# Delta attention: a new order of the engines' steps within the slots, and the transposed keys one slot sooner

## The chip, the cores and the metric

The kernel runs on one core of one Trainium2 chip. Its time is the device time of one execution in microseconds (us). The kernel before took 6605.63 us as the median of three runs (6602.77 to 6611.05). PE is TensorE, PEld its weight load, DVE VectorE, ACT ScalarE, POOL GpSimd.

## The reference, cut to what matters

The program computes four transformer layers on 2048 tokens of width 256, all in fp32, each with an attention and a feed-forward part. The change touches only the attention of layer 0, a gated delta rule with 16 heads of 128 x 128 state:

```python
q = short_conv(x @ Wq.T, conv_q); k = short_conv(x @ Wk.T, conv_k); v = short_conv(x @ Wv.T, conv_v)
v_hat = k @ Wsv.T; e = v_hat - v                        # statistics: |e|2, |e|1, cosine
beta = sigmoid(mlp_b(s)); amp = mlp_a(s)                # 3 -> 32 -> 1
g = -exp(A_log) * softplus(r * amp + dt_bias)           # decay of every key channel
...
def step(S, inp):
    S = S * exp(g_t)[..., None]
    delta = (v_t - k_t @ S) * b_t
    S = S + k_t[..., None] * delta[..., None, :]
    return S, q_t * scale @ S
...
o = rmsnorm(o) * norm_w * sigmoid(x @ Wg1.T @ Wg2.T + bg2);  return o @ Wo.T
```

## The kernel before, in words

`delta_attention` cuts the work into 64 units: a head times a group of 512 tokens, which is four chunks of 128. Units are software-pipelined. Each engine runs the same Python loop over slots `for g in range(SLOTS)`, and a new unit enters every `SL = 7` slots. `at(g, OFF)` says which unit has the step of offset `OFF` in slot `g`, so a step always falls on the same remainder of `g` by 7. I call these remainders slot 0 to slot 6. A unit passes through some 34 slots, so about five units are in work at once.

What runs in which slot (offset modulo 7):

- Projections K, V, Q on PE (L296): slots 0, 1, 2. ACT copies each out of the PSUM bank twice (L492, L493), and DVE adds the three other taps of the convolution (`convolve`, L680) in slots 1, 2, 3.
- Slot 4 silu; slot 5 values transposed (L328) and v_hat (L336), squares on ACT (L517 to L519, L582 to L584), errors on DVE (L764, L793); slot 6 the sums of squares on PE (`STAT`, L383); slot 0 `SUMS`, transposes of the sums (L431).
- Slot 1 `ROOT`: DVE copies the sums out (L704 to L706) and POOL takes a power of 128x20 numbers (L642). Slots 2, 3, 4: the small MLPs, on POOL and DVE.
- Slot 6 `Z`: PE spreads a and beta (L360, L366), DVE makes z and the scaled keys kF (L729, L737), ACT a softplus argument. Slots 0 and 1: DVE evaluates a polynomial (`horner`, L694). Slot 2 `KQ`: the decay (L527, L726), decayed keys and queries (POOL L635, DVE L740), their diagonal (L352, L752).
- Levels 0 to 6 in slots 3, 4, 5, 6, 0, 1, 2: the 128 x 128 triangular inverse is built by doubling. In each level PE forms `products` (L305), DVE masks them into MA (L691), POOL scales kq, kF and tot (`scale`, L614 to L616), PE multiplies (L396), ACT copies Xs (L569), PE multiplies again (L437, in the last level L439), DVE subtracts into Tm (L831), PE transposes Tm (L310) and ACT copies TT (L512). In level 0, Tm comes from a transpose (L451, L785), and two levels of `products` run in slot 3, one before and one behind `scale(ul, 0)`.
- Chunks k = 0 to 3 in slots 3 to 6, the recurrence: W (L341, reads the state St), R (DVE L770, ACT L508 for the first chunk of a sequence), D (L424), its copy Dl (ACT L552), S (L466) with O (L462, L467), and the new St (DVE L842 or L844). The S of chunk 0 also reads `khat`, the transposed keys (`KH`, PE L376, ACT L549), in slot 3.
- Slot 0 `OUT` (ACT L589, DVE L825, PE L476), slot 1 the root of the mean square (POOL L663), slot 3 `Y`, the output projection (PE L417) with its four copies on ACT (L560). Slot 3 `GATE`: the gate's matmul (L323), read by ACT in slot 4 (L544).

The order of the steps within a slot is the order in which the source has them; nothing reorders them afterwards. Each engine takes its instructions strictly in that order, so one that waits on a semaphore holds up all behind it. Weights come by DMA once for every four units, into two buffers.

Of the kernel before, what the change touches and what calls it, by code (L numbers as in the profile page):

```python
# [10 lines left out]
ALU = mybir.AluOpType  # L11
ACT = mybir.ActivationFunctionType
# [167 lines left out]
GATE_AT, KH_AT, CHUNK_AT, OUT_AT, RMS_AT, Y_AT = 17, 24, 24, 28, 29, 31  # L180
# [7 lines left out]
def delta_attention(nc, T, ins):  # L188
    with ExitStack() as c:
# [76 lines left out]
        with nc.Block() as block:  # L266
# [18 lines left out]
            def _(pe):  # L285
# [27 lines left out]
                for g in range(SLOTS):  # L313
# [4 lines left out]
                    if (u := at(g, GATE_AT)) is not None:  # L318
                        pe.wait_ge(evac[2], min(u + 3, NU0))
                        pe.wait_ge(z_ready, u + 1)  # L320
                        if u:
                            pe.wait_ge(tg_ready, u)
                        nc.tensor.matmul(fr[:, 1, :], w_of(u)[:, W_G2:W_END], g1T[:, tok(u):tok(u) + GRP], start=True, stop=True).then_inc(tg_mm, 1)  # L323
# [13 lines left out]
                    if chunk and not (first(uc) and k == 0):  # L337
                        if k == 0:
                            pe.wait_ge(scaled, 7 * uc + 7)
                        pe.wait_ge(s_ready, 4 * uc + k)  # L340
                        nc.tensor.matmul(ca[:, 0:P], kq[:, uc % 2, 0, ch_(k)], St[:, uc % 2], start=True, stop=True).then_inc(w_mm, 1)  # L341
                    if (u := at(g, K_AT)) is not None:
                        pe.wait_ge(*w_loaded(u))
                        if u:
                            pe.wait_ge(vtok_ready, u)
                        project(u, 1, W_K, 0)
                    if (u := at(g, KQ_AT)) is not None:
                        pe.wait_ge(kF_ready, u + 1)
# [93 lines left out]
                    if (u := at(g, V_AT)) is not None:  # L442
                        if u >= 2:
                            pe.wait_ge(z_ready, u - 1)
                        if u == 1:
                            pe.wait_ge(evac[2], 1)
                        project(u, 2, W_V, 1)
                    if level and lv == 0:
                        pe.wait_ge(mask0_ready, ul + 1)
                        for j in range(NC):  # L450
                            last = nc.tensor.transpose(xy[:, ch_(j)], MA[:, 0, ch_(j)], T.ident[:])  # L451
# [1766 lines left out]
```

## Time and profile before

| | |
|---|---|
| median of three runs | 6605.63 us |
| profiled execution, its own time | 6588.47 us |
| its span, first to last instruction | 6586.7 us |
| delta attention within it | about 24 to 3140 us |
| PE, PEld busy over the span | 92%, 67% |
| DVE, ACT, POOL busy over the span | 59%, 41%, 35% |
| mean granted TensorE clock | 0.959 of 2.4 GHz |

Busy time is the sum over the whole program, so its shares average over nine stages. For this change only the first half of the span matters, and in it the repeating unit: the same 7 slots come round 64 times. A timeline row gives the start, the length, the engine and the line, and in brackets how long the engine was idle before it and who ended that. A PE busy time is that of pipelined matmuls, whose ends are modelled, so the starts are the better clock.

### The profile page before, as it was taken

To read this page: it belongs to the slowest core of one execution; us is meant where nothing else is said; L and a number is where in the kernel's file an instruction comes from. 1 tells how busy PE (TensorE), PEld (TensorE's weight loads), DVE (VectorE), ACT (ScalarE), POOL (GpSimd) and SP (SyncE) were. 2 spreads that over 40 slices of the span, in tenths; PEclk is the share of its full clock that TensorE was granted. 3 is DMA by queue.
4 is the path that set the end of the run, shared out by engine and by line. 5 is a ranking of instruction groups with operands and counts; after the bars stand their busy time and mean duration, and the time that the engine had idled before them with its cause. 6 is when DMAs were issued, how large, how long until landed. Compare 5 with 4: busy or idle time off the path is not lost. (4 is left out here: it accounts for less than half of the span.)

```text
span 6586.7 us, 99233 instructions
## 1 busy us (share of the span) xinstructions
PE 6069.7 (92%) x37522; PEld 4392.9 (67%) x37522; DVE 3858.4 (59%) x7222; ACT 2708.2 (41%) x5584; POOL 2308.8 (35%) x2602
## 2 busy tenths in 40 slices
PE   5898989898889898988899999999999989999999
PEld 3777777777777777777477777653334667767665
DVE  5777777777777777775334444337654444444322
ACT  4445454545454444443145555413664122222211
POOL 3666667676666666675000000010000011111100
PEclk8999999999999999999999999998999999999999
DMA  0000000000000000000000000000001011211200
GB/s 29 5 5 5 3 2 5 5 5 5 5 5 1 5 5 5 5 1 1 15 18 14 12 11 12 23 7 1 1 1 52 1 62 62 68 68 68 75 7 7
DMA packets 33925, 112.56 MB, mean 17 GB/s; under 512 B 4272, under 2 KB 9648, under 8 KB 33456
## 3 DMA queue, kind: packets, MB, share of 16 engines
q1 hardware_dynamic: 33456, 106.22, 4.8%
q8 instruction: 305, 5.00, 0.3%
q14 instruction: 164, 1.34, 0.1%
HBM read 104.11 MB, written 2.10 MB: 16 GB/s over the span
## 5 line engine op out<-in xcount | busy, mean ns | idle before, releaser
L614 POOL TENSOR_TENSOR d_kq<-d_kq,d_tot 128x512 f32<-128x512 f32 x448 | 556.6, 1242 | 829.2 <-PE d_lpd L305 823.8
L305 PE MATMUL d_lpd<-d_kq,d_kF 128*128 128x128 f32 x3584 | 550.2, 302 | 110.9 <-POOL d_tot L616 103.3
L680 DVE SCALAR_TENSOR_TENSOR d_qkv<-d_raw,d_wts,d_qkv 128x512 f32<-128x512 f32 x576 | 506.8, 888 | 124.8 <-ACT d_qkv L493 120.0
L305 PEld LDWEIGHTS d_lpd<-d_kq,d_kF 128*128 128x128 f32 x3584 | 491.1, 211 | 133.1 <-POOL d_tot L616 126.5
L691 DVE COPY_PREDICATED d_MA<-d_pairs,d_lpd 128x512 f32<-128x512 int32 x384 | 316.4, 824 | 359.6 <-PE d_lpd L305 356.9
L396 PEld LDWEIGHTS d_xy<-d_Tm,d_MA 128*128 128x128 f32 x3072 | 409.4, 205 | 167.4 <-issue 165.7
L396 PE MATMUL d_xy<-d_Tm,d_MA 128*128 128x64 f32 x3072 | 434.8, 288 | 58.8 <-ACT d_TT L512 57.4
L1744 DVE TENSOR_REDUCE r_nm<-r_ps 128x2 f32<-128x1024 f32 x256 | 307.8, 1223 | 138.6 <-PE r_ps L1563 138.4
L994 POOL TENSOR_TENSOR f1rstd<-f1var,mhalf 128x4 f32<-128x4 f32 x4 | 4.0, 1009 | 1097.1 <-DVE f1var L1019 1097.1
L296 PE MATMUL d_fr<-xnT,d_wts 128*128 128x512 f32 x768 | 380.1, 618 | 0.7 <-ACT d_g1T L487 0.7
L437 PE MATMUL d_xy<-d_Xs,d_TT 128*128 128x64 f32 x2560 | 366.9, 293 | 0.2 <-ACT d_Xs L569 0.2
L1841 PE MATMUL e_pj<-xnT,e_wts 128*128 128x512 f32 x768 | 347.7, 602 | 13.5 <-DMA e_wts<-in_w3all 11.7
L437 PEld LDWEIGHTS d_xy<-d_Xs,d_TT 128*128 128x128 f32 x2560 | 358.4, 216 | 0.4 <-ACT d_Xs L569 0.4
L615 POOL TENSOR_TENSOR d_kF<-d_kF,d_tot 128x256 f32<-128x256 f32 x448 | 352.0, 786 | 0.0
L1664 ACT ACTIVATE r_pT<-r_ps 128x512 f32<-128x512 f32 x512 | 274.9, 598 | 146.3 <-PE r_ps L1571 145.7
L694 DVE SCALAR_TENSOR_TENSOR d_lp<-d_lp,d_ez 128x512 f32<-128x512 f32 x448 | 325.0, 725 | 13.1
L512 ACT ACTIVATE d_TT<-d_xy 128x256 f32<-128x256 f32 x320 | 124.5, 389 | 464.3 <-PE d_xy L310 464.3
L1304 DVE TENSOR_TENSOR c_sc<-c_sc,c_mask 128x128 f32<-128x128 f32 x256 | 76.7, 300 | 397.8 <-PE c_sc L1181 397.8
L1219 PEld LDWEIGHTS c_po<-c_pT,c_vt 128*128 128x128 f32 x2304 | 294.7, 191 | 21.0 <-ACT c_pT L1279 9.3
L1219 PE MATMUL c_po<-c_pT,c_vt 128*128 128x128 f32 x2304 | 301.9, 276 | 0.2
L1563 PE MATMUL r_ps<-r_kT,r_qT 32*128 32x512 f32 x1024 | 292.1, 694 | 2.7 <-DVE r_nm L1744 1.1
L642 POOL TENSOR_TENSOR d_pw<-d_st,d_half 128x20 f32<-128x20 f32 x64 | 257.5, 4024 | 98.6 <-DVE d_sums L706 98.5
(399 smaller groups left out, 13919.4 us busy)
## 6 DMA issues: line engine op xcount, KB each, us to landing
e_wts<-in_w3all SPq DMA_DIRECT2D x64, 897.0 KB, 4.6
d_wts<-in_headw SPq DMA_DIRECT2D x16, 583.5 KB, 3.8
c_wqo<-in_wqo SPq DMA_DIRECT2D x32, 256.0 KB, 2.6
f3ws<-in_f3w SPq DMA_DIRECT2D x17, 384.0 KB, 8.2
f2ws<-in_f2s SPq DMA_DIRECT2D x16, 256.0 KB, 6.6
f2qs<-in_f2q SPq DMA_DIRECT2D x16, 256.0 KB, 6.8
f1ws<-in_f1w SPq DMA_DIRECT2D x8, 384.0 KB, 6.4
f0ws<-in_f0w SPq DMA_DIRECT2D x6, 384.0 KB, 5.4
```

The costliest lines, as they stand in the source:

```text
L296: last = nc.tensor.matmul(fr[:, bank, :], w_of(u)[:, w0 + kd * P:w0 + (kd + 1) * P], T.xnT[:, kd, tok(u):tok(u) + GRP], start=(kd == 0), s ...
L305: last = nc.tensor.matmul(out[:, :, k], kF[:, u % 2, ch_(k)], moving[:, :, k, :, 1], start=True, stop=True)
L396: last = nc.tensor.matmul(mh(xy[:, j * 64:(j + 1) * 64], h), MA[:, lv, ch_(j)], even(Tm[:, ch_(j)], h), start=True, stop=True)
L437: last = nc.tensor.matmul(xy[:, 256 + j * 64:256 + (j + 1) * 64], TT[:, ul % 2, ch_(j)], Xs[:, j * 64:(j + 1) * 64], start=True, stop=True)
L614: nc.gpsimd.tensor_tensor(v, v, bc(bc(t_l[:, :, 0], 2, h), 1, 2), ALU.mult)
L615: nc.gpsimd.tensor_tensor(f, f, bc(t_l[:, :, 1], 2, h), ALU.mult)
L680: step = nc.vector.scalar_tensor_tensor(qkv[:, u % 3, x], raw[:, u % 2, x, i:i + GRP], tap(u, x, i), qkv[:, u % 3, x], ALU.mult, ALU.add)
L691: nc.vector.copy_predicated(into, bc(mh(pairs[:, lv], h), 1, 2), lpd[:].rearrange("p (x m h) -> p x m h", x=2, h=h)).then_inc(masked, 1)
L694: ch.link(nc.vector.scalar_tensor_tensor(lp[:], lp[:], LOG1P[i], ez[:], ALU.add, ALU.mult))
L1219: last = nc.tensor.matmul(po[:, 0:P], vt[:, n // (4 * QT) % 2, j], pT[:, n % 2, j * P:(j + 1) * P], start=(j == 0), stop=(j == t))
L1744: nc.vector.tensor_reduce(nm[:, t % 2, half, 4 * j + i0:4 * j + i0 + 2], ps[:, row_pair(row - 1):row_pair(row - 1) + 2], AX, ALU.max).then ...
L1841: last = nc.tensor.matmul(pj[:, x % 2, :], w[:, w0 + kd * P:w0 + (kd + 1) * P], T.xnT[:, kd, g * GRP:(g + 1) * GRP], start=(kd == 0), stop ...
```

## The change

`KH_AT` goes from 24 to 23: the four transposes of the scaled keys run in slot 2, behind the level 6 multiply and ahead of the projection of Q, and no longer in slot 3. ACT copies them out at the head of slot 3. All else moves steps within their slot. In each engine's loop the blocks stand in another order; their contents, waits, operands and buffers are as before. POOL's blocks move too, but since each runs in only one slot of the seven, the sequence of POOL's instructions comes out the same as before. No instruction is added or removed on any engine.

```diff
-GATE_AT, KH_AT, CHUNK_AT, OUT_AT, RMS_AT, Y_AT = 17, 24, 24, 28, 29, 31
+GATE_AT, KH_AT, CHUNK_AT, OUT_AT, RMS_AT, Y_AT = 17, 23, 24, 28, 29, 31
...
             def _(pe):
-                    if (u := at(g, GATE_AT)) is not None:
-                        pe.wait_ge(evac[2], min(u + 3, NU0))
...
+                    if (u := at(g, STAT_AT)) is not None:
+                        pe.wait_ge(kq_sq, u + 1)
+                        pe.wait_ge(err_sq, u + 1)
...
             def _(act):
-                    if (u := at(g, CHUNK_AT)) is not None:
-                        act.wait_ge(kh_mm, u + 1)
...
+                    if (u := at(g, Y_AT)) is not None:
+                        act.wait_ge(yo_mm, u + 1)
...
+                    if chunk:
+                        act.wait_ge(dl_mm, 4 * uc + k + 1)
+                        nc.scalar.activation(Dl[:, ch_(k)], ca[:, 0:P], ACT.Copy).then_inc(dl_ready, 1)
...
             def _(dve):
+                    if (u := at(g, K_AT + 1)) is not None:
+                        convolve(u, 1, 2)
...
                     if level and lv < 6:
                         mask(ul, lv + 1)
...
+                    if chunk:
+                        dve.wait_ge(s_mm, 4 * uc + k + 1)
...
+                    if (u := at(g, Z_AT)) is not None:
+                        nc.vector.tensor_tensor(kF[:, u % 2], qkv[:, u % 3, 1], fr[:, 2, :], ALU.mult).then_inc(kF_ready, 1)
```

The first place is DVE from the end of slot 6 through slot 0 into slot 1. Before, from the start of the polynomial (d_lp) to the second tap of K (d_qkv):

```order
L734 TENSOR_SCALAR d_lp<-d_ez 128x512
L694 SCALAR_TENSOR_TENSOR d_lp<-d_lp,d_ez 128x512 x3
L691 COPY_PREDICATED d_MA<-d_pairs,d_lpd 128x2x8x32
L825 SCALAR_TENSOR_TENSOR d_og<-d_tg,d_co 128x512
L694 SCALAR_TENSOR_TENSOR d_lp<-d_lp,d_ez 128x512
L831 TENSOR_TENSOR d_Tm<-d_Tm,d_xy 128x16x16
L704 TENSOR_SCALAR d_st<-d_fr 128x16
```

And now, where the line numbers are those of the changed file (L742 is L734, L817 is L825, L824 is L831):

```order
L742 TENSOR_SCALAR d_lp<-d_ez 128x512
L694 SCALAR_TENSOR_TENSOR d_lp<-d_lp,d_ez 128x512 x4
L691 COPY_PREDICATED d_MA<-d_pairs,d_lpd 128x2x8x32
L817 SCALAR_TENSOR_TENSOR d_og<-d_tg,d_co 128x512
L824 TENSOR_TENSOR d_Tm<-d_Tm,d_xy 128x16x16
L704 TENSOR_SCALAR d_st<-d_fr 128x16
```

The fourth step of the polynomial has moved from between d_og and d_Tm to ahead of the mask d_MA.

The second place is PE in slot 3 of a unit whose chunks carry a state over, from the last multiply of level 6 to the W of chunk 1. Before:

```order
L439 MATMUL d_xy<-d_TT,d_Xs 64x64 x4
L323 MATMUL d_fr<-d_g1T,d_wts 128x512
L341 MATMUL d_ca<-d_St,d_kq 128x128
L376 MATMUL d_fr<-ident,d_kF 128x128 x4
L305 MATMUL d_lpd<-d_kq,d_kF 128x2x64 x4
L417 MATMUL d_fr<-d_wo,d_og 128x256 x4
L424 MATMUL d_ca<-d_R,d_TT 128x128
L451 MATMUL d_xy<-ident,d_MA 128x128 x4
L305 MATMUL d_lpd<-d_kq,d_kF 128x2x64 x4
L462 MATMUL d_co<-d_kq,d_St 128x128
L466 MATMUL d_ca<-d_Dl,d_khat 128x128
L467 MATMUL d_co<-d_MA,d_Dl 128x128
```

And now, where L433 is L439, L369 is L341, L398 is L417, L405 is L424, L461 is L451:

```order
L414 MATMUL d_fr<-ident,d_kF 128x128 x4
L296 MATMUL d_fr<-xnT,d_wts 128x512 x2
L433 MATMUL d_xy<-d_TT,d_Xs 64x64 x4
L369 MATMUL d_ca<-d_St,d_kq 128x128
L305 MATMUL d_lpd<-d_kq,d_kF 128x2x64 x4
L398 MATMUL d_fr<-d_wo,d_og 128x256 x4
L405 MATMUL d_ca<-d_R,d_TT 128x128
L442 MATMUL d_co<-d_kq,d_St 128x128
L446 MATMUL d_ca<-d_Dl,d_khat 128x128
L447 MATMUL d_co<-d_MA,d_Dl 128x128
L461 MATMUL d_xy<-ident,d_MA 128x128 x4
L305 MATMUL d_lpd<-d_kq,d_kF 128x2x64 x4
```

The transposed keys (L414) now stand ahead of the projection of Q, and O and S of chunk 0 (L442 to L447) ahead of the second `products`. The gate's matmul, L477, is the next row behind these; it was the first of slot 3 (L323).

The third place is DVE in the same slot. Before, from the first mask to the new state:

```order
L749 COPY_PREDICATED d_MA<-d_pairs,d_lpd 128x256
L770 SCALAR_TENSOR_TENSOR d_R<-d_vtok,d_pw,d_ca 128x128
L777 TENSOR_TENSOR d_TT<-ident,d_MA 128x512
L782 COPY_PREDICATED d_MA<-d_pairs,d_lpd 128x256
L785 TENSOR_TENSOR d_Tm<-ident,d_xy 128x512
L680 SCALAR_TENSOR_TENSOR d_qkv<-d_raw,d_wts,d_qkv 128x512 x2
L691 COPY_PREDICATED d_MA<-d_pairs,d_lpd 128x2x128x2
L817 COPY d_raw<-d_raw 128x3x3
L844 SCALAR_TENSOR_TENSOR d_St<-d_St,d_tot,d_ca 128x128
```

And now:

```order
L716 COPY_PREDICATED d_MA<-d_pairs,d_lpd 128x256
L680 SCALAR_TENSOR_TENSOR d_qkv<-d_raw,d_wts,d_qkv 128x512
L737 COPY_PREDICATED d_MA<-d_pairs,d_lpd 128x256
L754 SCALAR_TENSOR_TENSOR d_R<-d_vtok,d_pw,d_ca 128x128
L680 SCALAR_TENSOR_TENSOR d_qkv<-d_raw,d_wts,d_qkv 128x512
L778 TENSOR_TENSOR d_TT<-ident,d_MA 128x512
L680 SCALAR_TENSOR_TENSOR d_qkv<-d_raw,d_wts,d_qkv 128x512
L798 TENSOR_TENSOR d_Tm<-ident,d_xy 128x512
L691 COPY_PREDICATED d_MA<-d_pairs,d_lpd 128x2x128x2
L830 SCALAR_TENSOR_TENSOR d_St<-d_St,d_tot,d_ca 128x128
L838 COPY d_raw<-d_raw 128x3x3
```

The three taps of Q (L680) are now strung between the masks and the two differences from the identity, and the copy of the halo (d_raw) stands behind the state.

## Rows read from the trace of the kernel before

**Rows 1.** Busy time and granted clock (PEclk) of four stretches, all engines.
```profile
400.00:2800.00 2400.00, 2158.92 (x14615) 1775.58 (x14616) 1845.17 (x3522) 1157.39 (x2343) 1640.89 (x1886) 0.94 0.01 4
1512.70:1519.50 6.80, 6.24 (x26) 5.75 (x27) 5.35 (x9) 0.77 (x2) 6.51 (x7) 0.50 0.01 2
1536.60:1540.00 3.40, 3.40 (x18) 3.40 (x17) 2.20 (x8) 1.72 (x4) 0.42 (x1) 0.50 0.04 10
1567.00:1656.00 89.00, 79.22 (x564) 63.84 (x564) 70.86 (x136) 45.26 (x92) 63.14 (x73) 1.00 0.03 8
```

**Rows 2.** What PE waited for, 400 to 2800 us: total, times, longest.
```profile
PE d_lpd L305 <- POOL d_tot L616: 81.8, 50, 2.6
PE d_xy L396 <- ACT d_TT L512: 43.9, 101, 0.6
PE d_ca L341 <- DVE d_St L842: 41.9, 25, 2.0
PE d_ca L341 <- DVE d_St L844: 38.4, 26, 1.9
PE d_xy L310 <- DVE d_Tm L831: 33.6, 51, 0.8
```

**Rows 3.** POOL's power, once in each unit: count, lengths, first and last start.
```profile
L642 POOL TENSOR_TENSOR d_pw<-d_st,d_half x64: 3523/4042/4044, 71.9 to 3030.3; 128x20 f32<-128x20 f32 x64
```

**Rows 4.** Timeline of one unit, slots 0 to 2: start, length, line, idle before.
```profile
1606.95 0.94 DVE L694 SCALAR_TENSOR_TENSOR d_lp<-d_lp,d_ez 128x512 f32<-128x512 f32 x1
1607.93 0.42 DVE L831 TENSOR_TENSOR d_Tm<-d_Tm,d_xy 128x256 f32<-128x256 f32 x1
1608.40 0.66 PE L310 MATMUL d_xy<-ident,d_Tm 128*128 128x128 f32 x4 [0.66 <-DVE d_Tm L831]
1608.66 4.04 POOL L642 TENSOR_TENSOR d_pw<-d_st,d_half 128x20 f32<-128x20 f32 x1 [0.70 <-DVE d_sums L706]
1609.62 1.08 PE L396 MATMUL d_xy<-d_Tm,d_MA 128*128 128x64 f32 x8 [0.56 <-ACT d_TT L512]
1613.53 0.41 DVE L831 TENSOR_TENSOR d_Tm<-d_Tm,d_xy 128x256 f32<-128x256 f32 x1
1614.10 0.60 PE L310 MATMUL d_xy<-ident,d_Tm 128*128 128x128 f32 x4
1615.89 1.08 PE L396 MATMUL d_xy<-d_Tm,d_MA 128*128 128x64 f32 x8 [0.30 <-ACT d_TT L512]
```

**Rows 5.** Timeline of the same unit, slot 3 and the head of slot 4.
```profile
1619.18 1.27 POOL L635 TENSOR_TENSOR d_kq<-d_qkv,d_tot 128x512 f32<-128x512 f32 x1
1619.28 1.12 PE L323 MATMUL d_fr<-d_g1T,d_wts 128*128 128x512 f32 x2
1620.41 0.72 POOL L646 TENSOR_TENSOR d_hid<-d_hid 128x256 f32<-128x256 f32 x1
1620.90 1.07 PE L305 MATMUL d_lpd<-d_kq,d_kF 128*128 128x128 f32 x8
1621.21 2.18 POOL L647 TENSOR_TENSOR d_hid<-d_hid,d_mlp 128x256 f32<-128x256 f32 x1
1621.40 1.40 DVE L680 SCALAR_TENSOR_TENSOR d_qkv<-d_raw,d_wts,d_qkv 128x512 f32<-128x512 f32 x2
1624.44 1.56 ACT L560 ACTIVATE d_y<-d_fr,d_rr 128x256 f32<-128x256 f32 x4
1626.84 0.38 PE L305 MATMUL d_lpd<-d_kq,d_kF 128*128 128x128 f32 x1 [2.18 <-POOL d_tot L616]
1628.29 1.29 DVE L691 COPY_PREDICATED d_MA<-d_pairs,d_lpd 128x512 f32<-128x512 int32 x1
1629.79 0.49 PE L341 MATMUL d_ca<-d_St,d_kq 128*128 128x128 f32 x2 [1.10 <-DVE d_St L844]
```

**Rows 6.** Timeline of the same unit, slots 5 and 6, the statistics.
```profile
1638.97 0.64 ACT L584 ACTIVATE d_sqs<-d_sqs 128x512 f32<-128x512 f32 x1
1641.48 1.92 PE L383 MATMUL d_fr<-d_sqs,d_pick 128*32 128x512 f32 x14
```

More of the change, by code:

```diff
@@ L441, in _ @@
                         last.then_inc(yt_mm, 1)
[L442 to L451, printed above, removed]
-                        last.then_inc(tr_mm, 1)
-                        pe.wait_ge(scaled, 7 * ul + 1)
-                        pe.wait_ge(masked, 7 * ul + 1)
-                        products(ul, 1)
                     if chunk:
@@ L477, in _ @@
                         last.then_inc(ss_mm, 1)
+                    if level and lv == 0:
+                        pe.wait_ge(mask0_ready, ul + 1)
+                        for j in range(NC):
+                            last = nc.tensor.transpose(xy[:, ch_(j)], MA[:, 0, ch_(j)], T.ident[:])
+                        last.then_inc(tr_mm, 1)
+                        pe.wait_ge(scaled, 7 * ul + 1)
+                        pe.wait_ge(masked, 7 * ul + 1)
+                        products(ul, 1)
+                    if (u := at(g, V_AT)) is not None:
+                        if u >= 2:
+                            pe.wait_ge(z_ready, u - 1)
+                        if u == 1:
+                            pe.wait_ge(evac[2], 1)
+                        project(u, 2, W_V, 1)
+                    if (u := at(g, GATE_AT)) is not None:
+                        pe.wait_ge(evac[2], min(u + 3, NU0))
+                        pe.wait_ge(z_ready, u + 1)
+                        if u:
+                            pe.wait_ge(tg_ready, u)
+                        nc.tensor.matmul(fr[:, 1, :], w_of(u)[:, W_G2:W_END], g1T[:, tok(u):tok(u) + GRP], start=True, stop=True).then_inc(tg_mm, 1)
                     if level and 1 <= lv < 6:
@@ L553, in _ @@
-                    if (u := at(g, Y_AT)) is not None:
-                        act.wait_ge(yo_mm, u + 1)
-                        act.wait_ge(rr_ready, u + 1)
-                        if u:
-                            act.wait_ge(y_added, 4 * u)
-                        for j in range(NC):
-                            bank = 2 if j < 2 else 3
-                            last = nc.scalar.activation(y[:, j // 2, (j % 2) * D:(j % 2 + 1) * D], fr[:, bank, (j % 2) * D:(j % 2 + 1) * D], ACT.Copy, scale=rr[:, j:j + 1])
-                        last.then_inc(y_read, 1)
```

327 lines of the change are left out of this document (160 added, 167 removed).

## The prediction, made blind

> **What bounds the kernel now.** I read four views. First the busy time by stretch: in the delta stage, 2400 us of it, PE is busy 2159 us, DVE 1845, POOL 1641, at a granted clock of 0.94; no engine is full, PE is nearest [rows 1]. Second POOL's power, which runs once in a unit and so measures the period: (3030.3 - 71.9) / 63 = 46.96 us for each of 63 periods [rows 3]. Third what PE waits for: 81.8 + 43.9 + 41.9 + 38.4 + 33.6 = 239.6 us in 2400, that is in 51.1 periods, so 4.7 us a period [rows 2]. The change adds and removes no work, so only these 4.7 us, new waits of the same kind, and the clock can move.
>
> Fourth the timeline of one unit at full clock. The waits are at three places, and each has an owner.
> - Slot 0 to 1: PE waits 0.66 us for Tm and 0.56 us for TT. The reader is to see that DVE's polynomial step L694 starts at 1606.95 and Tm only behind it, at 1607.93 [rows 4].
> - Slot 2: 0.30 us for TT [rows 4].
> - Slots 3 and 4: 2.18 us for POOL's `scale(ul, 0)`, then 1.10 us for the state St [rows 5]. POOL is a chain of its own here. It waits 0.70 us for the sums, starts the power at 1608.66 [rows 4], and from then on its next instructions follow closely, with kq (L635) at 1619.18, two MLP steps, and the scale that lets PE go at 1626.84 [rows 5]. So what starts the power late also makes the second `products` late, 18 us on.
>
> Of one unit's period the stretch from slot 0 to slot 4 is bound by POOL and DVE, and the rest, slots 4 to 6, by PE.
>
> **The change part by part.** All times are those of this unit, with minus for earlier.
>
> *Slot 0, the polynomial step goes ahead of the mask.* DVE idles there for the products anyway, so 0.94 us leave the path of Tm [rows 4]. Tm starts at about 1607.0, PE's L310 no longer waits (-0.66), the sums are ready some 0.9 sooner, and POOL's power starts when POOL is free, -0.7 (all its idle time). The 0.56 for TT stays: it is the copy between two dependent matmuls.
>
> *Slot 1, the third tap of K goes ahead of mask and Tm.* A tap is 0.70 us (1.40 for two) [rows 5]. DVE reaches slot 1 0.9 sooner and does 0.7 more before Tm, so Tm is ready at 1613.9 as before (1613.53 + 0.41 = 1613.94) while PE comes 0.65 sooner and has to wait. PE's L310 then starts at 1614.0 instead of 1614.10 [rows 4]: the first gain is spent here on a new wait of 0.55 us. It is not lost on ACT, which has V's copies out sooner and TT right behind, so the 0.30 wait of L396 in slot 2 goes, and L396 starts at about 1615.4 instead of 1615.89 [rows 4]: -0.5. The tap now runs beside the power instead of beside POOL's scale, a point for the next step.
>
> *Slots 2 and 3, before the first products.* Between L323 at 1619.28 and L305 at 1620.90 PE does three things in 1.62 us: the gate's matmul (about 1.0), W and the transposed keys [rows 5]. The keys move ahead by one slot and cost the same there; the gate goes behind the second products. PE could so start L305 at -0.5 - 1.0 = -1.5. It also needs POOL's kq, which ended at 1619.18 + 1.27 = 1620.45 [rows 5] and now ends 0.7 to 1.1 sooner. I take -1.1 for L305.
>
> *Slot 3 up to the second products.* POOL's two MLP steps follow kq, then the scale behind the first products. All of it starts 0.7 to 1.1 sooner. PE's own way there: L305 at 1619.8, 1.0 for it, 1.8 for Y, so Y ends at 1622.7. ACT now copies Y out (1.56 us [rows 5]) before Dl, so Dl is there at 1622.7 + 1.56 + 0.3 = 1624.6, S and O take to 1625.1, the transposes of MA to 1625.6. DVE on its side has its mask, three taps, both masks, R and TT done by about 1626.3, in time for Tm0. So the second products start at about 1625.7 by PE and between 1625.2 and 1626.1 by POOL, against 1626.84: -1.1.
>
> *Behind the second products.* Before, S and O stood there, and then PE waited 1.10 us until DVE had masked (1628.29, 1.29 us) and made St [rows 5]. Now S is long done, but DVE still makes St behind that mask, so W again starts 2.95 us behind the products (1629.79 - 1626.84). The gate's 1.0 us lies inside that wait, and costs nothing. Without that cover (if St came at once) it would cost its 1.0. W: -1.1. In half of the units the halo copy now follows St, and delays R instead; I count it at nothing.
>
> *Slots 4 to 6.* ACT's gate read goes behind Dl and Xs, DVE's St ahead of the beta steps: both can only help PE, by 0 to 0.2. PE's sums of squares go ahead of W and Z. They need ACT's last square, which ended at 1638.97 + 0.64 = 1639.61 while they ran at 1641.48 [rows 6]. Now they want to run 1.2 us sooner, at 1640.25, and ACT has the copy of the values (0.6) before the squares and no longer inside a wait: 1640.2. I charge +0.15. DVE's z comes 2 us later and kF 1.5 us later; both are used half a slot or more behind that, so I charge nothing; DVE's idle time before the products of slots 6 and 0 covers the move.
>
> *Sum.* -1.1 + 0.15 gives -1.0 us a period with rounding. Ends: -0.4 if products2 hang on Dl and port collisions, -1.7 if all of 0.66 + 0.30 and a good part of 2.18 go. Over 63 periods: -63 us (-25 to -107).
>
> *The clock.* The granted clock is 0.50, that is 1.2 GHz, at 1512.7 to 1519.5, behind the waits of slots 0 and 1, and at 1536.6 to 1540.0, behind those of slots 3 and 4; yet it is 1.00, 2.4 GHz, through 89 us that hold the same waits twice [rows 1]. So this idling is close to what tips it. A mean of 0.94 means (1 - 0.94) x 2 = 12% of the time at half clock, 5.6 us a period, worth 2.8 us. With 1.0 of 4.7 us of idling gone, and the rest more spread, I take a seventh of it, -0.4 a period, -25 us. Ends: +0.7 and -1.8 a period. The Trainium skill says the same in its own terms (TensorE: Matmul & The Clock Gate, What's actually happening): the slow clock is the default, and activity of the array lifts it.
>
> Together -88 us. The profiled execution took 6588.5 us, so 6500 for it; the median of the runs shown is 0.26% above it, at 6605.6, so the forecast for the median is 6518 us (-1.3%).
>
> **The rivals.**
>
> *Port collisions turn it slower.* MLP step L647 took 2.18 us with two taps of DVE beside it, its twin L646 0.72 [rows 5]: POOL stood still for both taps. The change puts all three taps between the first mask and Tm0, beside the scale that PE waits for, where before one of the heavy DVE operations ran. The Trainium skill has this as a rule (GPSIMD Engine Reference, Specifications): POOL's way into SBUF is shared with VectorE, and contention comes with DVE instructions that have two SBUF inputs; a tap has two. The trace agrees in this row. Worked out from rows: three taps hold the scale up by 2.1 us. If POOL gained 0.7 before and none of it by the tap of K, the second products start at +1.4, the taps that ran beside the next MLP steps give back 0.7 by slot 4, and Tm in slot 1 is no help: +0.7 to +1.0 a period, so 6605.6 + 50 = about 6656. It decides once POOL's scale ends behind 1626.8. Against it: the taps are only moved, the next steps of POOL have the port for themselves, and the tap of K has left POOL's chain for the power, which reads 20 columns.
>
> *The waits only change owners.* Dl behind four copies of Y, Tm in slot 1 and the squares in slot 6 eat the gain; for that they need 0.4 us each more than I gave. Then 6606 within noise, 6593 to 6619.
>
> *Half the sum.* Products2 hang on Dl, and the clock gives nothing: -0.5 a period, 6574.
>
> *The clock goes up.* If half of the slow stretches vanish, -1.4 comes on top of -1.0: -2.4 x 63 = -151, 6455. For it speaks the 89 us stretch; against it, that 3 us of waits still stand close together in slots 3 and 4.
>
> *It does not do what it says.* POOL's sequence is unchanged, though its source moved, so nothing comes from there; that is in the sum.
>
> **How the numbers follow.** Forecast (6480 to 6565) 0.50; clock 0.17; half the sum 0.11; owners change 0.10; slower 0.12. A measurement of this kernel tells 0.2%, 13 us, from no change. Faster by more: 0.50 + 0.17 + 0.11 = 0.78; within 0.10; slower 0.12. The range reaches to the clock's case and just to no change: 6440 to 6606.
>
> **What would show it.** Right: PE's wait for Tm in slot 0 gone and one of about 0.5 us at L310 in slot 1; L396 of slot 2 without wait; POOL's power without idle time before it; the second products about 6 us behind the first, but both earlier; PE's wait on `scale` below 1 us, and one for Dl in its place; the gate's matmul between the products and W. The period at 45.5 us. Wrong: POOL's three scale instructions in slot 3 together longer than 4 us; the sums of squares waiting over 0.5 us for ACT; a granted clock below 0.94.

## The result and the profile after

The changed kernel takes 6416.4 us, the median of 4 runs (6413.9 to 6419.3), against 6607.3 for the kernel before on the same chip: a ratio of 0.971 (95% interval 0.970 to 0.973), or 191 us less. The forecast was 6518 and its range ended at 6440, so the sign is right and the size is wrong by 102 us. The profiled span is 6412.1 us, 174.6 shorter than that of before; this is less than the 191 of the medians, since the profiled execution of before (6588.47 us) was faster than all four of its timed runs (6602.77 to 6611.05).

The same stretch of 2400 us answers to the first row of [rows 1]; the second row is one unit at full clock, the third a stretch that is mostly at half clock (0.50 from 1564.5 to 1567.5). Columns as there.

```profile
400.00:2800.00 2400.00, 2207.29 (x15582) 1786.41 (x15582) 1922.84 (x3756) 1226.07 (x2503) 1741.16 (x2014) 0.99 0.02 4
1341.14:1384.91 43.77, 40.82 (x292) 32.66 (x292) 35.43 (x71) 22.59 (x46) 31.93 (x37) 1.00 0.00 1
1564.80:1568.20 3.40, 3.40 (x19) 3.40 (x19) 3.33 (x5) 0.38 (x1) 3.15 (x4) 0.57 0.00 0
```

PE now gets through 15582 matmuls in the 2400 us where it did 14615, and the granted clock is 0.99 where it was 0.94. POOL's power, once a unit, is L631 here, and answers to [rows 3]:

```profile
L631 POOL TENSOR_TENSOR d_pw<-d_st,d_half x64: 3524/3973/3980, 72.5 to 2850.9; 128x20 f32<-128x20 f32 x64
```

(2850.9 - 72.5) / 63 = 44.10 us a period against 46.96, that is 2.86 x 63 = 180 us. The two profiled executions differ by 174.6 us in all, so the whole gain is in this loop.

The first five units are shorter than the rest in every kernel, so for all comparisons from here I use 53 steady units, from the power of the sixth to that of the 59th. Their mean is 47.36 us before ((2794.22 - 284.09) / 53) and 44.36 after ((2627.78 - 276.48) / 53). The trace also says in which of them the granted clock stayed at 1.00 throughout: 9 of the 53 before, with a mean of 45.48 us, and 34 after, with 43.96. This splits the 3.00 us a unit in two:

- **the path**, what a unit takes at full clock: 45.48 to 43.96, -1.52
- **the clock**, what the mean lies above that: 47.36 - 45.48 = 1.88 before, 44.36 - 43.96 = 0.40 after, -1.48

The units come in four kinds that take turns and differ by up to 0.5 us, and seven of the nine full units of before are of one kind. e5 and e6 below check this: there 51 and 53 units, of all kinds, stay at 1.00, and their means, 45.57 and 43.95, give -1.62 for the path.

What PE waits for, 400 to 2800 us (total, times, longest), answers to [rows 2]. L386 is the old L396, L369 is L341:

```profile
PE d_ca L446 <- ACT d_Dl L549: 66.8, 54, 1.7
PE d_xy L386 <- ACT d_TT L514: 35.6, 71, 0.6
PE d_ca L369 <- DVE d_St L830: 21.2, 28, 1.2
PE d_lpd L305 <- POOL d_kq L642: 16.9, 31, 0.8
PE d_ca L369 <- DVE d_St L828: 15.3, 23, 0.7
PE d_fr L398 <- DVE d_MA L820: 15.1, 31, 0.7
PE d_ca L405 <- DVE d_R L754: 11.2, 28, 1.0
PE d_xy L310 <- DVE d_Tm L824: 8.7, 37, 0.2
```

The 81.8 us for POOL's scale are gone and the 33.6 for Tm are 8.7. In their place stands Dl, 66.8 us. All rows make 190.8 us in 54.4 units, 3.5 a unit against 4.7: only 1.2 of the 2.9 us (46.96 - 44.10) show up as waits. The rest is mostly in the matmuls' own length: PE's busy time is 2207.29 / 54.4 = 40.6 us a unit where it was 2158.92 / 51.1 = 42.2, with the same matmuls. That is the clock.

A unit of the changed kernel at full clock, of the same kind as the one of [rows 4] (its chunks carry a state over), first slots 0 to 2:

```profile
1340.42 0.42 DVE L824 TENSOR_TENSOR d_Tm<-d_Tm,d_xy 128x256 f32<-128x256 f32 x1
1341.07 0.63 PE L310 MATMUL d_xy<-ident,d_Tm 128*128 128x128 f32 x4
1341.14 3.97 POOL L631 TENSOR_TENSOR d_pw<-d_st,d_half 128x20 f32<-128x20 f32 x1 [0.17 <-DVE d_sums L706]
1342.27 1.07 PE L386 MATMUL d_xy<-d_Tm,d_MA 128*128 128x64 f32 x8 [0.56 <-ACT d_TT L514]
1347.14 0.66 PE L310 MATMUL d_xy<-ident,d_Tm 128*128 128x128 f32 x4 [0.23 <-DVE d_Tm L824]
1348.53 1.08 PE L386 MATMUL d_xy<-d_Tm,d_MA 128*128 128x64 f32 x8
```

In slot 0 PE no longer waits for Tm, and POOL's idle time before the power is 0.17 us instead of 0.70. In slot 1 there is a new wait for Tm, 0.23 us. In slot 2 the wait for TT is gone. Slots 3 and 4, which answer to [rows 5]:

```profile
1351.13 1.60 POOL L642 TENSOR_TENSOR d_kq<-d_qkv,d_tot 128x512 f32<-128x512 f32 x1
1352.68 1.47 POOL L666 TENSOR_TENSOR d_hid<-d_hid 128x256 f32<-128x256 f32 x1
1352.78 1.18 PE L305 MATMUL d_lpd<-d_kq,d_kF 128*128 128x128 f32 x8
1354.22 1.99 PE L398 MATMUL d_fr<-d_wo,d_og 128*128 128x256 f32 x8 [0.27 <-DVE d_MA L820]
1355.04 1.83 POOL L614 TENSOR_TENSOR d_kq<-d_kq,d_tot 128x512 f32<-128x512 f32 x1
1356.26 1.57 ACT L530 ACTIVATE d_y<-d_fr,d_rr 128x256 f32<-128x256 f32 x4 [2.78 <-PE d_fr L398]
1356.47 0.49 PE L405 MATMUL d_ca<-d_R,d_TT 128*128 128x128 f32 x2 [0.25 <-DVE d_R L754]
1356.83 1.28 POOL L615 TENSOR_TENSOR d_kF<-d_kF,d_tot 128x256 f32<-128x256 f32 x1
1357.69 0.29 ACT L549 ACTIVATE d_Dl<-d_ca 128x128 f32<-128x128 f32 x1
1358.08 1.06 POOL L616 TENSOR_TENSOR d_tot<-d_tot 128x256 f32<-128x256 f32 x1
1358.13 0.46 PE L446 MATMUL d_ca<-d_Dl,d_khat 128*128 128x128 f32 x2 [0.95 <-ACT d_Dl L549]
1359.19 1.18 PE L305 MATMUL d_lpd<-d_kq,d_kF 128*128 128x128 f32 x8
1360.21 1.02 PE L477 MATMUL d_fr<-d_g1T,d_wts 128*128 128x512 f32 x2
1360.41 1.32 DVE L691 COPY_PREDICATED d_MA<-d_pairs,d_lpd 128x512 f32<-128x512 int32 x1
1361.52 0.32 DVE L830 SCALAR_TENSOR_TENSOR d_St<-d_St,d_tot,d_ca 128x128 f32<-128x128 f32 x1
1361.89 0.49 PE L369 MATMUL d_ca<-d_St,d_kq 128*128 128x128 f32 x2 [0.67 <-DVE d_St L830]
```

PE now waits 0.95 us for Dl, which stands on ACT behind four copies of Y. The second products follow without a wait, the gate's matmul L477 lies behind them, and W waits 0.67 for St instead of 1.10. The end of the unit, slots 6 and 0 of the next (answers to [rows 6]):

```profile
1371.27 0.65 ACT L578 ACTIVATE d_sqs<-d_sqs 128x512 f32<-128x512 f32 x1
1372.17 1.92 PE L328 MATMUL d_fr<-d_sqs,d_pick 128*32 128x512 f32 x14
1384.84 0.63 PE L310 MATMUL d_xy<-ident,d_Tm 128*128 128x128 f32 x4
```

The same end in the kernel before:

```profile
1653.91 0.66 PE L310 MATMUL d_xy<-ident,d_Tm 128*128 128x128 f32 x4 [0.66 <-DVE d_Tm L831]
```

So the two like units can be laid side by side. Each time is the distance from PE's L310 of slot 0 (1608.40 before, 1341.07 after, 1608.40 - 0.66 = 1607.74 in the forecast):

| to the start of | before | forecast | after |
|---|---|---|---|
| L310, slot 1 | 5.70 | 6.26 | 6.07 |
| L396/L386, slot 2 | 7.49 | 7.66 | 7.46 |
| first products | 12.50 | 12.06 | 11.71 |
| second products | 18.44 | 18.00 | 18.12 |
| W of chunk 1 | 21.39 | 20.95 | 20.82 |
| L310, slot 0 of the next unit | 45.51 | 44.5 | 43.77 |

Up to W the forecast holds within 0.35 us everywhere, and within 0.13 at W. What it missed on the path lies behind W: 24.12 us before, 22.95 after.

### The profile page after: what moved, and what is told of

It is laid out like the page before. It is cut to its first block and busy times, and to the rows that moved or that the text cites. A ratio compares the mean times of both kernels' runs of the same rounds, so it can differ in the third digit from the quotient of the medians.

```text
span 6412.1 us, 99259 instructions
## 1 busy us (share of the span) xinstructions
PE 5966.7 (93%) x37522; PEld 4274.2 (67%) x37522; DVE 3802.8 (59%) x7222; ACT 2693.9 (42%) x5584; POOL 2292.0 (36%) x2602
## 5 line engine op out<-in xcount | busy, mean ns | idle before, releaser
L680 DVE SCALAR_TENSOR_TENSOR d_qkv<-d_raw,d_wts,d_qkv 128x512 f32<-128x512 f32 x576 | 530.5, 921 | 53.2 <-ACT d_qkv L493 46.2
L305 PE MATMUL d_lpd<-d_kq,d_kF 128*128 128x128 f32 x3584 | 521.0, 290 | 33.4 <-POOL d_kq L642 26.7
L305 PEld LDWEIGHTS d_lpd<-d_kq,d_kF 128*128 128x128 f32 x3584 | 459.0, 199 | 58.5 <-POOL d_kq L642 34.7
L386 PEld LDWEIGHTS d_xy<-d_Tm,d_MA 128*128 128x128 f32 x3072 | 389.0, 196 | 93.9 <-issue 92.4
L386 PE MATMUL d_xy<-d_Tm,d_MA 128*128 128x64 f32 x3072 | 406.8, 277 | 44.8 <-ACT d_TT L514 44.8
L296 PE MATMUL d_fr<-xnT,d_wts 128*128 128x512 f32 x768 | 364.3, 597 | 0.7 <-ACT d_g1T L487 0.7
L431 PE MATMUL d_xy<-d_Xs,d_TT 128*128 128x64 f32 x2560 | 331.2, 274 | 0.0
L431 PEld LDWEIGHTS d_xy<-d_Xs,d_TT 128*128 128x128 f32 x2560 | 320.7, 197 | 0.0
L694 DVE SCALAR_TENSOR_TENSOR d_lp<-d_lp,d_ez 128x512 f32<-128x512 f32 x448 | 310.9, 694 | 13.2
L1183 PE MATMUL c_sc<-c_kT,c_qT 128*128 128x512 f32 (+3 forms) x768 | 290.2, 487 | 0.7 <-ACT c_qT L1247 0.7
L631 POOL TENSOR_TENSOR d_pw<-d_st,d_half 128x20 f32<-128x20 f32 x64 | 253.9, 3967 | 72.4 <-DVE d_sums L706 72.4
```

The lines of the kernel that those rows point to most:

```text
L296: last = nc.tensor.matmul(fr[:, bank, :], w_of(u)[:, w0 + kd * P:w0 + (kd + 1) * P], T.xnT[:, kd, tok(u):tok(u) + GRP], start=(kd == 0), s ...
L305: last = nc.tensor.matmul(out[:, :, k], kF[:, u % 2, ch_(k)], moving[:, :, k, :, 1], start=True, stop=True)
L386: last = nc.tensor.matmul(mh(xy[:, j * 64:(j + 1) * 64], h), MA[:, lv, ch_(j)], even(Tm[:, ch_(j)], h), start=True, stop=True)
L431: last = nc.tensor.matmul(xy[:, 256 + j * 64:256 + (j + 1) * 64], TT[:, ul % 2, ch_(j)], Xs[:, j * 64:(j + 1) * 64], start=True, stop=True)
L680: step = nc.vector.scalar_tensor_tensor(qkv[:, u % 3, x], raw[:, u % 2, x, i:i + GRP], tap(u, x, i), qkv[:, u % 3, x], ALU.mult, ALU.add)
L694: ch.link(nc.vector.scalar_tensor_tensor(lp[:], lp[:], LOG1P[i], ez[:], ALU.add, ALU.mult))
```

## The experiments

Times are medians; the ratio is to the kernel before, measured beside it. "Steady", "full" and "clock" are the mean unit, the unit at full clock and their difference, as defined above. They come from the one profiled execution of each kernel, which for before was some 18 us faster than the median and for e1 12 us slower (the others within 10), so in a usual run of before the clock's loss is probably a little above 1.88.

| kernel | median us | ratio (95%) | steady | full | clock |
|---|---|---|---|---|---|
| before | 6605 to 6613 | 1 | 47.36 | 45.48 | 1.88 |
| changed | 6416.4 | 0.971 (0.970-0.973) | 44.36 | 43.96 | 0.40 |
| e1 keys alone | 6654.8 | 1.007 (1.005-1.009) | 48.55 | 45.49 (3 units) | 3.06 |
| e2 PE and keys | 6705.8 | 1.016 (1.014-1.017) | 49.19 | 46.68 (2 units) | 2.5 |
| e3 DVE | 6485.4 | 0.983 (0.981-0.984) | 45.70 | 44.33 | 1.37 |
| e4 ACT | 6614.0 | 1.001 (0.999-1.002) | 47.42 | 45.39 | 2.03 |
| e5 before, fillers | 6482.9 | 0.981 (0.979-0.983) | 45.64 | 45.57 | 0.07 |
| e6 changed, fillers | 6386.2 | 0.966 (0.965-0.968) | 43.95 | 43.95 | 0.00 |
| e7 changed, Dl first | 6413.0 | 0.970 (0.969-0.972) | 44.38 | 43.95 | 0.43 |
| e8 changed, h3 back | 6568.8 | 0.994 (0.992-0.995) | 46.88 | 44.86 | 2.02 |
| e9 before, h3 alone | 6462.7 | 0.979 (0.977-0.980) | 45.26 | 44.79 | 0.47 |
| e10 changed, fillers, MA first | 6386.8 | 0.967 (0.965-0.968) | 43.91 | 43.91 | 0.00 |
| e11 h3 back, fillers | 6495.9 | 0.986 (0.981-0.991) | 45.69 | 44.85 | 0.84 |
| e12 PE, keys, DVE | 6546.9 | 0.991 (0.990-0.993) | 46.51 | 45.60 | 0.91 |
| e13 changed, PE as before | 6429.0 | 0.973 (0.971-0.975) | 44.42 | 44.30 | 0.12 |
| e14 keys alone, fillers | 6485.4 | 0.981 (0.979-0.983) | 45.68 | 45.57 | 0.11 |

**Is it the clock? (e5, e6)** Matmuls of 128x128 whose results nobody reads fill PE's waits; those in slots 0 and 1 stand behind one more semaphore wait, and nothing else is changed. In e5 there are thirteen: six ahead of the second products, three ahead of chunk 1's W, two at the wait for Tm in slot 0 and two at the wait for TT in slot 1. In e6 there are eight: four ahead of O and S of chunk 0 in slot 3, where PE waits for Dl, two ahead of W and two at the wait for TT in slot 1. The diff has two of e5's four places.

```diff
+                        if k == 1:
+                            for _ in range(3):
+                                nc.tensor.matmul(co[:, 384:512], T.ident[:], T.ident[:], start=True, stop=True)
...
+                        for _ in range(6):
+                            nc.tensor.matmul(co[:, 384:512], T.ident[:], T.ident[:], start=True, stop=True)
```

> The kernel before, with 13 matmuls more in each unit (128x128, fp32, about 0.24 us each) that write a part of PSUM nobody reads: 6 ahead of the second products in slot 3, 3 ahead of W in slot 4, 2 ahead of the transposes in slot 0, 2 ahead of the multiply in slot 1. They lie inside PE's waits of 2.18, 1.10, 0.66 and 0.56 us, so they change no chain. Theory (the slow clock follows from PE's idling, and the changed kernel got half of its gain that way): the granted clock of 400 to 2800 us goes from 0.94 to 0.98 or more, and the period by -1.4 us, to the 45.4 us that the periods without a slow stretch have: ratio 0.984 to 0.989. Rival (the clock only follows the path; the slow stretches cost nothing that the waits don't hide): ratio 1.000 to 1.005, as the extra work costs a little.

> The changed kernel, with 8 matmuls more in each unit that write a part of PSUM nobody reads: 4 ahead of O and S of chunk 0 in slot 3, 2 ahead of W in slot 4, 2 ahead of the multiply in slot 1. Theory of the clock: it still has 1.2 us of half clock a period, so -0.3 us a period at most, ratio to before 0.967 to 0.970, and a clock of 1.00. Rival: the fill delays O and S: 0.972 to 0.976.

The stretch of 2400 us in e5, and PE's longest wait there:

```profile
400.00:2800.00 2400.00, 2277.48 (x16501) 1880.76 (x16500) 1942.18 (x3651) 1198.17 (x2425) 1730.41 (x1955) 1.00 0.01 4
```

```profile
PE d_lpd L305 <- POOL d_tot L629: 41.6, 39, 1.2
```

Useless work makes the kernel before some 125 us faster. Its granted clock goes from 0.94 to 1.00, and its steady unit to 45.64 us, 0.16 above what it took at full clock anyway (45.48). So 1.7 of its 47.36 us were lost to the clock, and the path hardly moved. It gained somewhat more than expected (0.984 to 0.989), the rival of no gain fell. e6 does the same to the last 0.40 of the changed kernel (clock 1.00 in all 53 units), and is 30 us faster than it, a little more than expected (0.967 to 0.970).

**One DVE instruction (e8, e9).** e9 is the kernel before with the fourth polynomial step (h3) ahead of the mask; e8 is the changed kernel with it back between og and Tm.

```diff
+                    if (u := at(g, POLY_AT)) is not None:
+                        horner(u, 3)
                     if level and lv < 6:
                         mask(ul, lv + 1)
```

> The changed kernel, with the fourth step of the polynomial back between og and Tm in slot 0, as before the change. Theory: PE waits 0.66 us for Tm again and POOL's power starts 0.7 us later; at full clock +0.6 us a period, and idling that comes back brings slow stretches: +1.0 to +2.0 us a period, ratio to before 0.981 to 0.990. Rival (slot 0 is spent again in slot 1, as the forecast had it): +0.1 us, ratio 0.972 to 0.974.

> The kernel before with one instruction moved: DVE's fourth polynomial step (d_lp, L694) of slot 0 stands ahead of the mask and no longer between d_og and Tm. Theory (this step frees the power, and what it frees is kept and lifts the clock): PE's wait for Tm in slot 0 and the power's idle time go; 0.5 to 0.9 us a unit at full clock (45.49 to about 44.8) and 1 to 2 us of slow clock a unit less; about 6510, between 6470 and 6560. Theory of the forecast (slot 1 spends slot 0's gain on a new wait): here slot 1 is as before, without the tap of K ahead of Tm, so the gain arrives anyway, but small: 0.5 a unit, 6575. Rival (one step alone can't help, since the second products still stand where they were and POOL's collision with the taps eats it): 6600, no change.

e9, the stretch and what PE waits for:

```profile
400.00:2800.00 2400.00, 2168.81 (x15284) 1768.94 (x15286) 1925.06 (x3686) 1213.71 (x2453) 1732.93 (x1977) 0.98 0.01 4
```

```profile
PE d_lpd L305 <- POOL d_tot L616: 113.4, 53, 2.6
PE d_ca L341 <- DVE d_St L842: 43.1, 26, 2.0
PE d_xy L396 <- ACT d_TT L512: 41.1, 106, 0.6
PE d_ca L341 <- DVE d_St L844: 28.1, 27, 1.9
```

e8's three longest waits in total (its granted clock in the same stretch is 0.95):

```profile
PE d_ca L446 <- ACT d_Dl L549: 55.0, 52, 1.7
PE d_xy L386 <- ACT d_TT L514: 41.3, 93, 0.6
PE d_xy L310 <- DVE d_Tm L824: 36.6, 59, 0.7
```

This one instruction, alone, gives 142 of the 191 us; taken back out of the changed kernel it costs 152. On the path it is worth 0.69 us (e9) and 0.90 (e8): about the length of PE's wait for Tm, which is gone from e9's list. The wait for POOL's scale grew there, from 1.6 to 2.1 us a unit. By the clock it is worth twice as much, 1.41 and 1.62.

The traces also say where in a unit the half clock begins. I cut the 53 steady units into windows of 0.5 us and call windows in a row with a granted clock below 0.9 one slow stretch. In all kernels of this table they begin at two places only: within 3.5 us of the start of POOL's power, which is at the waits of slots 0 and 1, or 17 to 26 us behind it, which is at those of slots 3 and 4.

| kernel | slow stretches from slots 0 and 1 | from slots 3 and 4 | clock, us a unit |
|---|---|---|---|
| before | 40 | 17 | 1.88 |
| e9 before, h3 alone | 0 | 27 | 0.47 |
| changed | 16 | 3 | 0.40 |
| e8 changed, h3 back | 45 | 0 | 2.02 |
| e1 keys alone | 42 | 50 | 3.06 |
| e3 DVE | 4 | 31 | 1.37 |
| e13 changed, PE as before | 1 | 9 | 0.12 |
| e11 h3 back, fillers | 22 | 0 | 0.84 |

So in e9 the one instruction took away every slow stretch that began in slots 0 and 1, though the 0.56 us wait for TT stayed there, and behind the waits of up to 2.6 us for POOL, which stayed too, only 13 begin. The 27 of e9 last 3.6 us in the mean, the 57 of before 5.1. Both theories had the direction: e9's 6463 lies just outside of its bounds (6470 to 6560), and e8's ratio of 0.994 outside of 0.981 to 0.990, as the step is worth more than either allowed. The other expectations, 6575 and 6600 for e9 and 0.972 to 0.974 for e8, fell.

**Does PE's new order matter? (e2, e12, e13)** e2 gives the kernel before PE's new loop and `KH_AT = 23`; e12 DVE's loop as well; e13 is the changed kernel with PE's old loop (keys still in slot 2).

> The changed kernel's PE loop and KH_AT = 23, with the loops of ACT and DVE as before. Theory (POOL chain and DVE's place of St set the period, PE's order frees the first products from the gate and the keys and hides the gate behind the second): products earlier by 0.5 to 1.0 us, and Dl is copied ahead of Y so that S is early; but the wait for Tm in slot 0 and the late sums stay. -0.7 us a period and a little clock, ratio 0.985 to 0.993. Rival (PE's order alone is the gain): the ratio of the changed kernel, 0.971.

> The kernel before with the changed PE order, the transposed keys in slot 2 and the changed DVE order, but ACT's order as before. DVE alone gave 0.9825, PE with the keys 1.0155, ACT alone 1.0008; all together 0.9712. Theory (the gate's matmul out of slot 3 and S and O ahead of the second products help only when DVE gives R and Tm0 soon; ACT adds little): 6430 to 6450, ratio about 0.975. Rival (ACT's Dl behind the tanh and the keys' copy holds S up, so the new PE order needs ACT's new order): 6480 to 6530, no better than DVE alone. Third: the effects add up, 0.998, 6590.

> The changed kernel with PE's order as before; the keys stay in slot 2. DVE's order alone gave 0.9825, PE with keys and DVE 0.9914, all together 0.9712. Theory (PE's order is worth something once ACT fits it): this loses S and O ahead of the second products and has the gate's matmul back ahead of the first: 0.3 to 0.6 us a unit, 6440 to 6470, ratio 0.975 to 0.98. Rival (DVE and ACT carry all, PE's order is worth nothing): 6416 within 10. Second rival (keys in slot 2 cost clock as they did alone): 6500.

The longest waits of PE, 400 to 2800 us, in e2, e12 and e13, in this order:

```profile
PE d_ca L405 <- DVE d_R L770: 67.0, 73, 2.7
```

```profile
PE d_xy L431 <- ACT d_Xs L569: 77.8, 52, 1.5
```

```profile
PE d_lpd L305 <- POOL d_tot L616: 92.1, 42, 2.5
PE d_ca L341 <- DVE d_St L830: 43.8, 28, 2.5
```

PE's order with the moved keys makes a unit 1.2 us longer at full clock (by two full units only): PE now stands at chunk 0's R, up to 2.7 us, which DVE makes late. Both expectations for e2 had a gain and fell. With DVE's order (e12) that wait falls to 20.2 us, and PE waits for ACT's Xs, 1.5 us each time. It is always in slot 6, and a row of e12's timeline shows why:

```profile
1019.76 0.72 ACT L533 ACTIVATE d_mz<-d_z,d_wts 128x512 f32<-128x512 f32 x1 [3.69 <-DVE d_z L789]
```

In ACT's old order the three steps of the softplus argument stand ahead of Dl and Xs, and DVE's new order makes their z late (ACT's longest wait for it was 1.5 us in the kernel before); in ACT's new order they stand behind Xs. All three expectations for e12 fell (6430 to 6450, 6480 to 6530, 6590). With all three orders, PE's is worth 0.34 us on the path, and e13 loses only 12.6 us to the changed kernel, since its clock is the better one (0.12 against 0.40); its 6429 lies between the two expectations, 6440 to 6470 and 6416 within 10. So PE's order is not what made the kernel faster. ACT's new order, worth nothing alone (e4), gives 130 us once PE's and DVE's are taken: from e12 to the changed kernel only ACT's loop differs, since POOL's instructions come in the same sequence in both.

**Keys, DVE and ACT alone (e1, e3, e4, e14).** e1 is one number; e14 is e1 with e5's fillers.

```diff
-GATE_AT, KH_AT, CHUNK_AT, OUT_AT, RMS_AT, Y_AT = 17, 24, 24, 28, 29, 31
+GATE_AT, KH_AT, CHUNK_AT, OUT_AT, RMS_AT, Y_AT = 17, 23, 24, 28, 29, 31
```

> The kernel before, with KH_AT = 23 alone: the transposed keys in slot 2, every order within the slots as before. Theory (the period is set by POOL's chain from the power to its scale in slot 3, and PE is only late at its own waits): in slot 3 the keys stood ahead of the first products but kq from POOL was ready just before those, so the move by itself gives PE 0.4 us it then spends waiting for POOL: 0 to -0.3 us a period, ratio 0.997 to 1.000. Rival (the keys are the large part of the gain, as the first products start the chain to St): -1.5 us a period, ratio 0.985.

> The kernel before with the transposed keys in slot 2, and the thirteen filler matmuls of e5 (their results are never read). Keys alone took 45.49 us a unit at full clock, as before, but 48.12 in the mean. Theory (the keys' loss is clock alone): with fillers as fast as e5, 6483, ratio 0.981, within 10 us. Rival (it lengthens the path of PE in slot 2 where nothing shows it): 6520 to 6560.

> The changed kernel's DVE loop, with PE, ACT and KH_AT as before. Theory: the wait for Tm in slot 0 (0.66 us) and POOL's 0.7 us before the power go, the tap of K leaves POOL's chain, St no longer waits for the halo copy: -1.0 us a period at full clock, and with less idling of PE at slots 0 and 1 some slow stretches go: ratio 0.978 to 0.988. Rival (the three taps of Q beside POOL's scale cost what the first step gives): ratio 0.995 to 1.005.

> The changed kernel's ACT loop, with PE, DVE and KH_AT as before. Theory: ACT is idle more than half of the time and its order only turns who waits; the copy of Dl behind the four copies of Y costs nothing, since S stands behind the second products: ratio 0.998 to 1.002. Rival (ACT's order holds S up by 1.5 us, so St and W are late): ratio 1.01.

The stretch in e1 and in e14:

```profile
400.00:2800.00 2400.00, 2202.78 (x14223) 1827.04 (x14223) 1765.45 (x3423) 1125.81 (x2286) 1605.33 (x1836) 0.89 0.01 4
```

```profile
400.00:2800.00 2400.00, 2282.20 (x16515) 1877.18 (x16514) 1939.53 (x3648) 1193.71 (x2429) 1728.33 (x1955) 1.00 0.02 4
```

The keys in slot 2 cost the kernel before 0.7%, and nothing of it is path: at full clock a unit takes 45.49 us with them and 45.48 without (three units and nine), and with the clock held up the kernel is as fast as e5, 6485.4 against 6482.9, as e14's theory had it. The loss was in neither expectation for e1. The table above shows where it lies: 50 slow stretches from slots 3 and 4 instead of 17, of which 43 begin 18 to 21 us behind the power, right behind the wait for POOL's scale, where none begins before, though that wait is as long as before. DVE's whole order, within what was expected of e3, is worth 1.15 us on the path, yet e3 is slower than e9 with its one instruction, by 23 us, because its clock is worse (1.37 against 0.47). ACT's order alone is worth nothing, as expected.

**Smaller ones (e7, e10, e11).** e7 moves chunk 0's Dl on ACT ahead of the four copies of Y. e10 is e6 with DVE's diagonal MA (L820) ahead of V's third tap. e11 is e8 with e6's fillers.

```diff
+                    if chunk and k == 0:
+                        act.wait_ge(dl_mm, 4 * uc + k + 1)
+                        nc.scalar.activation(Dl[:, ch_(k)], ca[:, 0:P], ACT.Copy).then_inc(dl_ready, 1)
                     if (u := at(g, Y_AT)) is not None:
```

> The changed kernel, with ACT's copy Dl of chunk 0 ahead of the four copies of Y. PE waits 1.24 us a period for Dl there. Theory (behind Dl the second products wait for POOL's scale, which ends at about the same time): 0.3 to 0.8 us of the wait turns into one for POOL, -0.4 us a period, ratio to before 0.965 to 0.970. Rival (POOL's scale is not the next limit): -1.2 us a period, ratio 0.959. Other rival: no change, 0.971, since the second products are bound by POOL already.

> The changed kernel with the eight filler matmuls of e6 (their results are never read) and DVE's diagonal d_MA (L820) ahead of V's third tap in slot 2. Theory: Y's wait of 0.7 us for d_MA goes, but the second products stand behind Dl and so only half of it arrives: 0.1 to 0.2 us a unit below e6's 6386: about 6376. If the path to the second products is POOL's kq and scale alone, Y's wait was covered: 6386, same as e6. If V's tap now beside kq costs POOL time: 6400.

> e8 (the changed kernel with the fourth polynomial step back between d_og and Tm) with the eight filler matmuls of e6. e8 took 44.89 us a unit at full clock and 46.52 in the mean, the changed kernel 43.98 and 44.10. Theory (the step is worth 0.9 us a unit by the path, and the rest, 1.5, by the clock alone): with the clock held up the unit takes 44.9 to 45.1, so about 6450 to 6460, some 65 above e6. Rival (the slow clock is no consequence of idle time but costs what it costs, or the whole 2.4 us are path): 6560 as e8. If the clock is half held: 6500.

Two rows of e7's list of waits:

```profile
PE d_lpd L305 <- POOL d_tot L619: 34.4, 38, 1.2
...
PE d_ca L446 <- ACT d_Dl L525: 18.5, 54, 0.5
```

The wait for Dl falls from 66.8 to 18.5 us, and the one for POOL's scale comes back with 34.4: Dl and the scale end together, and the earlier Dl is worth nothing by itself. That was the second rival of e7. The earlier diagonal MA in e10 is worth nothing either: 6386.8 against 6386.2, so Y's wait for it was covered. In e11 the path is as predicted (44.85), but e6's fillers hold the clock only partly: they stand in slots 1, 3 and 4, and not where e11 waits for Tm in slot 0.

```profile
PE d_xy L310 <- DVE d_Tm L834: 46.4, 82, 0.7
PE d_xy L393 <- ACT d_TT L524: 6.9, 23, 0.3
```

The wait for TT in slot 1 is filled, the one for Tm is open, and all 22 slow stretches of e11 begin there. So its 6496 is the expected case of a clock half held (6500), between the theory (6450 to 6460) and the rival (6560). One of its four runs took 6556.6 us and the others 6489 to 6497, so this median is less sure than the rest.

## Why the prediction was wrong, step by step

- **Slot 0, right.** The wait of 0.66 us for Tm goes, and POOL's power starts with the sums (idle 0.17 and not 0.70).
- **Slot 1, right in kind, half in size.** A new wait of 0.55 us was forecast at L310; it is 0.23. From slot 0 to slot 1 PE takes 0.37 us more than before, where 0.56 was forecast, and the gain of the TT wait in slot 2 brings it back to even (7.46 against 7.49).
- **First and second products, W: right.** -1.1 us each was forecast. Counting slot 0's 0.66, they measure -1.45, -0.98 and -1.23. Dl takes the place of POOL's scale, and the gate hides in W's wait. A wait of Y for the diagonal MA (0.27 us here) was not forecast; e10 shows that it costs nothing.
- **Slots 4 to 6, wrong in sign.** I charged +0.15 for the sums of squares. PE does not wait for ACT there at all: the last square ends at 1371.92, and L328 starts at 1372.17. From W to the next L310 the unit gains 1.17 us; 0.66 of it is the Tm wait of the next slot 0, so slots 4 to 6 give 0.51. It comes in pieces of 0.1 to 0.2 us a slot; the largest is between W and slot 5's multiply (6.34 to 6.15). No experiment takes these apart. This unit gains 1.74 us. The mean is -1.52, since one kind of unit in four takes 44.3 us. Forecast was -1.0, with -1.7 as the end.
- **The clock, the step that failed.** "With 1.0 of 4.7 us of idling gone, and the rest more spread, I take a seventh of it, -0.4 a period": it was -1.48 of 1.88, four fifths. I had computed the cost of the half clock from the rows, 2.8 us a period (somewhat too much: fillers win back 1.7), and I had seen that this idling is close to what tips it; but I then scaled the loss with the idle time, as if it were proportional. It is not. e9 has about the same idle time as before (230 us in the list against 240) and loses 0.47 instead of 1.88; e13 has 229 and loses 0.12. e1 waits less, 194 us, and loses 3.06. So it matters where the waits stand. Of the 57 slow stretches before, 40 begin at the pair of Tm (0.66) and TT (0.56) in slots 0 and 1. e9 removes the wait for Tm and none is left there; e8 brings it back, and 45 begin there; e11 keeps Tm and fills TT, and 22 do. But Tm is not all: the changed kernel has only the TT wait there, as e9 has, and still 16. What else about their places decides is not settled here; a run that fills one wait at a time would say more. The rival "the clock goes up" was the case that came; at 6455 it had the clock's part right (-1.4), and it missed by the path's.
- **The rival of POOL's port** did not come. One of its signs did: the three scale instructions of slot 3 take from 1355.04 to 1359.14, 4.10 us and so more than 4. POOL's steps beside the taps are long too (L666 1.47 us where the same step, L646, took 0.72, kq 1.60 against 1.27 [rows 5]), but L667, the old L647 with its 2.18, is down to 0.73, and the scale ends just when PE gets to the second products: they start at 1359.19, without a wait. Counted from the L310 of slot 0 the scale ends 1.0 us earlier than the 1626.8 which that rival needed.

In the forecast's own terms, over 63 periods, the clock was missed by 1.08 us a period, 68 us, and the path by 0.52, 33 us; together these are the 102 us that it missed, but for rounding. The bigger step that failed is thus the clock's term, and the path's was right in its mechanism up to W and too small behind it.

The measured terms, -1.52 - 1.48 = -3.00 us, make -159 us over the 53 steady units. The ten other periods add 21, and the rest of the program is 5 longer: that is the 174.6 between the two profiled executions. The 16 us up to 191 are the profiled execution of before, which was faster than its runs.

## What to carry to other kernels

Split a period into the unit at full clock and what the mean lies above it, before pricing a move; where the second part is not small, fill PE's waits with dummy matmuls once, to see at what price the clock comes back. That one run here would have given the forecast the size of its clock term, and the eight fillers are worth 30 us even behind the changed order. And before an order of four engines is rewritten, move the single instruction that stands ahead of the one PE waits for: here it was three quarters of the whole.

## What was not expected of the hardware

- PE is 90% busy in the stretch before, with no single wait above 2.6 us, and still has a granted clock of 0.94. The Trainium skill (TensorE: Matmul & The Clock Gate, A second HAM failure mode: psum-queue depth-cycling) has a case in which short idling between groups of matmuls makes the clock swing between its two levels; these rows agree (0.50 in two of the stretches of [rows 1], 1.00 in the last).
- The granted clock is not a function of the idle time. In 2400 us, 194 us of listed waits go with a clock of 0.89 (e1), some 230 with 0.98 (e9) and with 0.99 (e13), 190.8 with 0.99 (the changed kernel).
- POOL's power on 20 columns took 3.53 us in e9 and 4.04 in the kernel before, with the same instruction. In e9 it starts 0.2 us ahead of DVE's tap and not 0.1 behind it; that this is the cause is not shown.
